# Chunk attention: value matmuls of a step issued in four double visits instead of eight single ones

## What is computed

```
Q, K, V = (x @ W.T).reshape(H, b, s, 8)       # H = 16, b = 16, s = 512
scores  = einsum('hbqd,hbkd->hbqk', Q, K)
out     = einsum('hbqk,hbkd->hbqd', softmax(scores), V).reshape(b, s, -1)
y       = out + x                             # x is the row-normalised input
return (y - mean(y)) / sqrt(var(y) + eps)     # over a whole batch item
```

## Time and profile before

| | us |
|---|---|
| median of 3 runs | 4279.96 |
| lowest and highest | 4271.9, 4286.19 |
| span of the profiled execution | 4275.1 |
| chunk attention within it, to its last value matmul | 0 to 901.7 |
| TensorE busy over the span | 3658.2 (86%) |
| VectorE busy | 2761.7 (65%) |
| ScalarE busy | 2243.4 (52%) |

### The profile page before, as it was taken

How to read it: one execution, slowest core, us unless ns; L and a number is a source line. 1 busy time by engine, 2 the same in 40 slices (tenths; PEclk the granted TensorE clock), 3 DMA queues, 4 the chain that set the end, 5 groups by cost and what they waited for, 6 DMA issues and landing times. The chain is left out here.

```text
span 4275.1 us, 89510 instructions
## 1 busy us (share of the span) xinstructions
PE 3658.2 (86%) x31167; PEld 2189.1 (51%) x31167; DVE 2761.7 (65%) x6182; ACT 2243.4 (52%) x5440; POOL 1942.7 (45%) x1927
## 2 busy tenths in 40 slices
PE   6999999965959999999999999997666777797768
PEld 1333333324935555555555555556664566575546
DVE  6888888845446666666666666655455665565465
ACT  2666666742415555555555555553225554475367
POOL 2222222117426666656665666656541121466075
PEclk7999999975979999999999999995788998797979
DMA  5333333312642111111111111112452222110000
GB/s 97 57 57 58 59 58 61 50 33 65 209 129 49 40 42 44 45 41 40 44 44 43 40 41 45 44 32 73 153 179 54 67 70 51 35 61 6 1 1 40
DMA packets 418239, 252.25 MB, mean 59 GB/s; under 512 B 251186, under 2 KB 344354, under 8 KB 416642
## 3 DMA queue, kind: packets, MB, share of 16 engines
q1 hardware_dynamic: 409156, 228.56, 23.0%
q0 software_dynamic: 8640, 17.97, 1.3%
HBM read 75.12 MB, written 41.75 MB: 27 GB/s over the span
## 5 line engine op out<-in xcount | busy, mean ns | idle before, releaser
L2495 POOL TENSOR_TENSOR ra_prob<-ra_prob,ra_inverse 128x256 f32<-128x256 f32 (+3 forms) x512 | 639.6, 1253 | 636.2 <-DVE ra_inverse L2689 478.4
L2651 ACT ACTIVATE ra_prob<-ra_ps_s,ra_low 128x128 f32<-128x128 f32 (+3 forms) x1024 | 534.0, 530 | 739.6 <-DVE ra_low L2663 739.5
L2311 DVE TENSOR_REDUCE ca_mx<-ca_ps_s 128x2 f32<-128x1024 f32 x512 | 600.9, 1212 | 111.6 <-PE ca_ps_s L2172 111.2
L2237 ACT ACTIVATE ca_pT<-ca_ps_p 128x512 f32<-128x512 f32 x1024 | 547.8, 601 | 220.5 <-PE ca_ps_p L2182 218.6
L2663 DVE TENSOR_REDUCE ra_low<-ra_ps_s 128x2 f32<-128x256 f32 (+3 forms) x512 | 408.2, 818 | 310.7 <-PE ra_ps_s L2577 309.6
L2172 PE MATMUL ca_ps_s<-ca_kst,ca_qst 128*128 128x512 bf16 x1024 | 395.6, 392 | 37.2 <-DVE ca_mx L2311 20.9
L2519 PE MATMUL ra_ps_t<-ident,ra_prob 128*128 128x128 f32 x2560 | 364.2, 281 | 44.3 <-ACT ra_probT L2629 36.4
L2182 PE MATMUL ca_ps_p<-ca_qst,ca_kst 128*128 128x512 bf16 x1024 | 386.1, 382 | 4.0 <-ACT ca_pT L2237 3.9
L2519 PEld LDWEIGHTS ra_ps_t<-ident,ra_prob 128*128 128x128 f32 x2560 | 273.3, 141 | 213.6 <-ACT ra_probT L2629 83.5
L2577 PE MATMUL ra_ps_s<-ra_kz,ra_qz 64*128 64x128 f32 (+3 forms) x2048 | 381.0, 470 | 0.0
L2591 PE MATMUL ra_ps_o<-ra_probT,ra_v 128*64 128x512 f32 (+3 forms) x2048 | 331.7, 445 | 0.0
(11 more groups left out here) (411 smaller groups left out, 7272.0 us busy)
## 6 DMA issues: line engine op xcount, KB each, us to landing
moe_w_own<-moe_w1T SPq DMA_DIRECT2D x142, 256.0 KB
ra_qz<-ra_rot SPq DMA_DIRECT2D x512, 64.0 KB, 2.0
ra_kz<-ra_rot SPq DMA_DIRECT2D x512, 64.0 KB, 2.0
ca_kst<-ca_bounce SPq DMA_DIRECT2D x256, 64.0 KB
ca_bounce<-ca_thirds SPq DMA_DIRECT2D x192, 64.0 KB, 3.0
ca_qst<-ca_bounce SPq DMA_DIRECT2D x64, 192.0 KB
moe_hs<-moe_rows SPq DMA_DIRECT2D x142, 66.0 KB
moe_raw<-in_L_ffn_W SPq DMA_DIRECT2D x32, 256.0 KB, 2.9
```

The lines of the kernel that those rows point to most:

```text
L2237: nc.scalar.activation(pT[:, (NS * hp + u) % PRING, :], ps_p[n % NP][:], ACT.Exp).then_inc(sg["drained"], 1)
L2311: nc.vector.tensor_reduce(mx[:, hm % 2, 2 * j:2 * j + 2], ps_s[m % 2][:].rearrange("p (b k) -> p b k", b=2), AX.X, ALU.max)\
L2495: nc.gpsimd.tensor_tensor(at, at, inverse[:, n % PROB, 2 * tile:2 * tile + 2].unsqueeze(2).broadcast_to([P, 2, keys]), ALU.mult)\
L2651: nc.scalar.activation(prob[:, score % PROB, t, head, 0:keys], part(score, t)[:, head, :], ACT.Exp, bias=low[:, score % PROB, at:at + 1], ...
```

## The change

The eight visits of a step are issued in twos. Visits 6 and 7 of a half stand together behind position 3 of the step after, visits 0 and 1 behind position 11, 2 and 3 behind 19, 4 and 5 behind 27. Before, they stood one by one behind positions 7, 11, 15, 19, 23, 27, 31 and 3. The first of each two moves back by four positions; the second stays where it was. No instruction is added or removed, no other engine's code is changed, and the semaphore counts are the same.

```diff
                         if u == 3 and hl is not None:
+                            values(6, hl)
                             values(7, hl)
-                        if hp is not None and u % 4 == 3 and u >= 7:
-                            values((u - 7) // 4, hp)
+                        if hp is not None and u % 8 == 3 and u >= 11:
+                            values((u - 11) // 4, hp)
+                            values((u - 11) // 4 + 1, hp)
```

## The result

The changed kernel took 4318.87 us (median of 4 runs, 4315.65 to 4329.11), the kernel before in the same comparison 4277.32 (4271.9 to 4286.19). The ratio is 1.0097, 95% interval 1.0078 to 1.0116: slower by 0.97%, 41 us. I had forecast 4316 and 36 us more.

What follows compares the result with a forecast made beforehand. TensorE sets the pace, coupled to VectorE by two pair buffers; a step loses 1.93 us more and saves 0.88, 1.05 longer; 29.4 + 3.7 + 2.7 = 35.8 us gives 4316, range 4298 to 4344.

Steps and rivals of the forecast that it cites:

- What bounds the kernel: Attention step of 26.13 us: TensorE sets the pace, VectorE a close second; coupled waits lose 1.26 us a step.
- What a join saves: Value visits on TensorE: a visit costs 1.08 us alone, 0.86 following another; four joins save 0.88 us a step.
- The rival without a saving: Joined visits save nothing, since four column groups must be filled again: 28 us more, 4344; 12 in 100.
- What a join costs: Runs of eight positions: the third pair must wait for VectorE's two buffers; a step loses 1.93 us more.
- the walk: Follows each run of eight positions from the matmul after the visits: 3.19 us lost a step against 1.26.
- The steps without the front part: Steps 32 and 33, without statistics, normalisation or projections: 1.87 us longer each, 3.7 in both.
- The steps without scores: Steps 34 and 35, TensorE waiting for ScalarE's exponentials: 5.18 against 4.80 us, 0.38 for each of seven runs, 2.7.
- The sum for the attention: Attention steps together: 29.4 + 3.7 + 2.7 = 35.8 us longer.
- Where VectorE idles: VectorE's idle time gathers in fewer, longer pieces of some 1.3 us or more behind the joined visits.
- The rival that VectorE's 3.1 us of slack would cover the new waits: VectorE's idle time in a step absorbs the added 1.93 us, only the saving stays: 28 us faster, 4252; 6 in 100.

## Why the prediction was right

- What bounds the kernel: right, and shown. With short reductions 1.46 us of the 26.13 go.
- What a join saves, 0.22 by two rows of the rope attention: right. The joined visits take 2.17 from scores to matmul, 2.16 forecast. Four column groups join as two do. The rival without a saving is out.
- What a join costs: each place of the walk has its row. Positions 4 to 11 lose 0.49 + 0.77 = 1.26 (forecast 1.22), 12 to 19 0.67 (0.66), 20 to 27 0.94 (0.91), 28 to 3 0.40 (0.40). That is 3.27 against 1.26 before, 2.01 more; less four joins of 0.22 it gives 1.13, and the step is 27.20 - 26.13 = 1.07 longer, 1.05 forecast. The 0.06 is of the size that rounding of so many subtracted starts can give.
- The steps without the front part: from its turn to the next, step 32 is 1.88 us longer (1.87 forecast), and step 33, whose stretch ends in a step without scores, 1.21 (1.87).
- The steps without scores: two runs of eight in the changed kernel start their visits 5.22 apart, forecast 5.18, before 4.80.

```profile
900.59 1.92 PE L2192 MATMUL ca_ps_o<-ca_pT,ca_vst 128*32 128x512 f32 x16
...
905.81 1.93 PE L2192 MATMUL ca_ps_o<-ca_pT,ca_vst 128*32 128x512 f32 x16
```

- The sum for the attention was 35.8 us and 35.0 was measured. The other 7 of the 41.9 us of span lie behind it, in code that is the same. From the last value matmul to the end are 3373.4 us before and 3380.3 after; in the traces of the experiments with the turn at 8 or 16, with the same code there, it lies between 3371.3 and 3384.7, and in the two kernels with the turn at 12, which ran beside a 4297.19 of the kernel before, at 3394.7 and 3395.5. It varies by more than 7 with nothing changed in it, so I count it as spread and not as an effect; its source stays open. The forecast of 36 us is for the attention alone, and the 41 of the whole runs are that and 6 or 7 us of this spread.
- Where VectorE idles: wrong in part. I had it idle behind the second of two visits, in pieces of some 1.3 us or more. One piece in a step is like that, 2.39; the others are 0.54 or less. What costs time is what the walk uses, that both buffers are empty when TensorE resumes and the third pair then has to wait, and not the idleness itself.
- The rival that VectorE's 3.1 us of slack would cover the new waits fell for the reason given: the slack did not shrink, it is 98.3 us (81.0 + 17.3) for 81.6, but it lies where no buffer is full.
- What I had not seen: with the reduction out of the way the turn in the middle of the long run is next, and then ScalarE's banks at its end. And a part of the loss belongs to the place: four equal joins are not four equal costs.

## What to carry to other kernels

The two engines coupled by two buffers ran better here when the faster one's scores came in short, even runs. In a run of scores TensorE is the faster one here (0.86 us a pair for VectorE's 1.12), though it is the busier one over a step. Work of the faster engine that the slower one doesn't need (here the value matmuls) was worth spreading between the coupled pieces, even if each break costs 0.2 us. Walk the queue with the durations of the trace from one resumption to the next: ready, length, release. For the change itself it came within 0.04 us in each run of positions. It failed where an item was left out: the statistics in VectorE's queue (0.37 and 0.43 us a step), and the turn and ScalarE's banks once the reductions were short (0.55). Spread such breaks over the places that have no other pause, and not evenly by count: that was worth 22 us here by the medians, 0.3 to 0.6% by the interval.

## What the runs showed of the hardware

The row of a small matmul is not its cost. The turn's row is 0.27 us long, but the scores behind it start 0.11 after it when nothing holds them (515.51 to 515.62 and 519.24 to 519.35 above). So the losses behind the turn that are given here, 0.45 and 0.77, are each 0.16 short; their difference is not.

A visit in four column groups (128x32, float32, 512 columns) that follows another costs 2.17 - 1.30 = 0.87 us and 1.08 alone: about 0.2 us for leaving the neighbouring matmuls and coming back. These are 128x128 and bfloat16, the visits neither, so what the shape alone costs was not separated. The Trainium skill says (TensorEngine Tiling (Array Packing), Key Properties) that changing the tiling mode drains TensorE; the runs agree with it, but the change, which leaves half as many blocks of value matmuls between the others, was slower all the same.
